# Another order for ScalarE's silu, gelu, sums and evictions in the first feed-forward of a four-stage block

## The reference

```python
def bitlinear158(x, w, b):
    xq = act_quant(rms_norm(x))          # 8-bit integers per row
    wq = weight_quant(w)                 # -1, 0, 1 times a scale
    return einsum('bsd,od->bso', xq, wq) + b
h = silu(bitlinear158(x, w1, b1))        # 512 -> 2048
h = gelu(h, approximate=False)
h = layer_norm(h, ln_g, ln_b)
return bitlinear158(h, w2, b2)           # 2048 -> 512
```

## Time and profile before

| | us |
|---|---|
| median of 3 runs | 903.49 (903.21 to 906.27) |
| the profiled execution | 903.19 |
| its span in the trace | 901.4 |
| busy: PE / DVE / ACT / POOL | 673.6 / 678.6 / 610.7 / 325.6 |

### The profile page before, as it was taken

How to read it: one execution, slowest core, us unless ns; L and a number is a source line. 1 busy time by engine, 2 the same in 40 slices (tenths; PEclk the granted TensorE clock), 3 DMA queues, 4 the chain that set the end, 5 groups by cost and what they waited for, 6 DMA issues and landing times. The chain is left out here.

```text
span 901.4 us, 14255 instructions
## 1 busy us (share of the span) xinstructions
PE 673.6 (75%) x5262; PEld 371.7 (41%) x5262; DVE 678.6 (75%) x1140; ACT 610.7 (68%) x814; POOL 325.6 (36%) x355
## 2 busy tenths in 40 slices
PE   5853056767857757779989978899998377979785
PEld 2421023333423323446655545556355144545452
DVE  1569879999999997885893797556442488989983
ACT  2788459998977894588982886489362055656574
POOL 0012611446295556371671265113031023323332
PEclk9985578999887898679999998999999798989999
DMA  8800030000000000622320121123000000000001
GB/s 320 329 1 0 17 124 0 1 1 1 0 1 1 0 1 2 209 65 96 95 66 28 34 65 45 33 69 107 0 2 1 33 1 12 25 24 23 24 36 47
DMA packets 21761, 43.70 MB, mean 48 GB/s; under 512 B 3905, under 2 KB 8513, under 8 KB 20801
## 3 DMA queue, kind: packets, MB, share of 16 engines
q1 hardware_dynamic: 21696, 42.85, 13.8%
HBM read 38.61 MB, written 4.19 MB: 47 GB/s over the span
## 5 line engine op out<-in xcount | busy, mean ns | idle before, releaser
L1460 DVE TENSOR_REDUCE c_nmax<-c_s 128x1 f32<-128x384 f32 (+3 forms) x176 | 108.7, 633 | 83.5 <-PE c_s L1670 83.5
L1572 ACT ACTIVATE c_probs<-c_e 128x512 f32<-128x512 f32 (+1 forms) x176 | 94.5, 558 | 57.8 <-PE c_e L1700 56.8
L1395 POOL TENSOR_TENSOR c_psum<-c_probs 128x1536 f32<-128x1536 f32 x16 | 55.9, 3492 | 156.4 <-ACT c_probs L1572 156.4
L1168 PE MATMUL b_y<-w2q,b_q2T 128*128 128x512 bf16 x256 | 72.5, 438 | 51.4 <-ACT b_q2T L1093 25.8
L2098 PE MATMUL d_gu<-gateq,d_xqT 128*128 128x352 bf16 x512 | 93.1, 332 | 13.8 <-DVE d_h L1899 12.7
L1667 PE MATMUL c_s<-c_kT,c_qaT 96*128 96x128 f16 (+3 forms) x256 | 73.4, 320 | 22.5 <-DVE c_nmax L1460 20.2
L1142 PE MATMUL b_up<-shared,b_xqT 128*128 128x512 bf16 x256 | 73.5, 414 | 2.4 <-ACT b_h L1059 2.4
L1698 PE MATMUL c_e<-c_qaT,c_kT 98*128 98x512 f16 (+3 forms) x256 | 69.7, 306 | 3.3 <-ACT c_qaT L1559 2.8
L2027 ACT ACTIVATE d_sg<-d_gu,d_dq 128x352 f32<-128x352 f32 x64 | 35.4, 554 | 52.2 <-PE d_gu L2098 52.2
L2098 PEld LDWEIGHTS d_gu<-gateq,d_xqT 128*128 128x128 bf16 x512 | 49.4, 103 | 50.0 <-DVE d_h L1899 19.0
L1168 PEld LDWEIGHTS b_y<-w2q,b_q2T 128*128 128x128 bf16 x256 | 25.6, 108 | 90.0 <-issue 36.5
(11 more groups left out here) (232 smaller groups left out, 1836.0 us busy)
## 6 DMA issues: line engine op xcount, KB each, us to landing
c_stage<-in_gateT SPq DMA_DIRECT2D x16, 704.0 KB, 4.0
c_stage<-in_downT SPq DMA_DIRECT2D x6, 768.0 KB, 4.7
xs<-in_x SPq DMA_DIRECT2D x4, 1024.0 KB, 17.3
a_wf<-in_w1T SPq DMA_DIRECT2D x2, 2048.0 KB, 16.0
a_wf<-in_w2T SPq DMA_DIRECT2D x2, 2048.0 KB, 20.9
out<-xs SPq DMA_DIRECT2D x16, 256.0 KB, 2.0
a_ctxT<-in_ctxT SPq DMA_DIRECT2D x1, 1024.0 KB, 4.9
b_ln_g<-in_ln_g SPq DMA_DIRECT2D x1, 1024.0 KB, 4.8
```

What stands on the lines that cost most here:

```text
L1168: last = nc.tensor.matmul(y_ps[:], q2T[:, n % 2, c, :], w2q[:, c, :], start=(c == 0), stop=(c == IC - 1))
L1395: nc.gpsimd.tensor_tensor(psum[:], region(slot, 0)[:, :, P:], region(slot, 1), ALU.add).then_inc(psum_ready, 1)
L1460: nc.vector.tensor_reduce(nmax[:, G % 2, i, n:n + heads], s_ps[u % 2][:, 0:heads * (i + 1) * P].rearrange("p (n k) -> p n k", n=heads), ax ...
L1572: nc.scalar.activation(probs[:, G % 2, at:at + width], e_ps[fill % 3][:, 0:width], ACT.Exp).then_inc(e_read, 1)
```

## The change

In ACT's loop over the pairs the same steps are called in another order. Before gelu(n) stand now both halves of silu(n) and both of silu(n+1), with squares(n-2) and first_half(n-2) between the latter. gelu(n+1) follows spread(n) directly, and squares(n-1) and gather(n+2) come behind it. No step is added or taken out, and no other stream changes.

```diff
@@ -1099,15 +1099,15 @@
                 n = 2 * p
                 silu(n, 0)
                 silu(n, 1)
+                squares(n - 2)
+                silu(n + 1, 0)
+                first_half(n - 2)
+                silu(n + 1, 1)
                 gelu(n)
-                squares(n - 2)
-                first_half(n - 2)
                 spread(n)
-                silu(n + 1, 0)
+                gelu(n + 1)
                 squares(n - 1)
                 gather(n + 2)
-                silu(n + 1, 1)
-                gelu(n + 1)
                 spread(n + 1)
                 first_half(n - 1)
                 if p == 7:
```

## The result

| | before | after |
|---|---|---|
| median of 8 runs of each, us | 904.09 (903.21 to 910.78) | 910.75 (907.56 to 912.47) |
| ratio after to before, 95% interval | | 1.0057 (1.0029 to 1.0084) |
| profiled execution / its span, us | 903.19 / 901.4 | 912.47 / 910.7 |
| stage length, us | 240.02 | 246.11 |
| ahead of the stage / behind it, us | 119.17 / 542.21 | 122.90 / 541.69 |

A forecast was written before the change was run, and what follows sets the result against it. DVE was taken as the bound, with ACT running ahead of it. Start +3.34, middle -0.38 and last tiles +0.98 gave +3.94, so +4.0 on 903.49: 907.5 us, 0.44% slower; 8-in-10 range 903.3 to 910.8.

The forecast's parts named there:

- ACT's relief is worth 0: Pair loop: 16 table loads fewer, 20.5 us off ACT, booked as 0 because DVE is the bound.
- The start: Tile 0: gelu(0) 4.32 us later behind tile 1's silus; DVE enters the full loop 3.34 us late at affine(1).
- The middle: Tiles 2 to 13: new loop DVE to PE to ACT booked 0; two old deviation waits go, -0.4 (-0.38 in the sum).
- slack at slope(12): Tile 12's turn: gelu's mean ready at 300.07, DVE there at 302.09, so 2.0 us of slack.
- slope(14): Tiles 14 and 15: DVE newly waits 1.54 us for the mean; +0.98 us left by affine(15).
- The tail: Chain from spread(15) to the last two projections: shifts by the same 0.98 us as affine(15).
- rival C: Up projections on PE at 1.2 GHz make the new loop bind in more turns: +6 to +10, say 910.5 us; chance 0.22.
- +4.0: Whole kernel: the summed delay, +3.34 - 0.38 + 0.98 = +3.94, rounded, in us.
- 5.9: Upper bound of the delay in us, 4.32 + 1.54, with no old wait recovered; more only by rival C.
- The total: Whole kernel: 903.49 + 4.0 = 907.5 us, 0.44% slower.
- the forecast's own range: Whole kernel: 906.2 to 908.9 us for the main forecast, which had chance 0.60.
- within 0.5%: Whole kernel: change too small to tell, under 4.5 us (line at 908.0); share 0.52, against 0.41 slower and 0.07 faster.

The follow-up runs named there:

- e5: Kernel before, old order, with Silu in place of Gelu, leaving one table load; computes something else. Ratio to before 0.9961, stage 240.32 us.
- e1: Changed kernel with the old order in the first pair only. Ratio to before 1.0063, stage 243.94 us.
- e2: Kernel before with the new order in the first pair only. Ratio to before 1.0031, stage 243.35 us.
- e4: Changed kernel with the old order in the first and last pair, new in the six between. Ratio to before 1.0006, stage 242.51 us.
- e9: As e4, but gather(n+2) ahead of squares(n-1) in the six middle pairs. Ratio to before 1.0001, stage 240.51 us.
- e8: Changed kernel with 22 spare matmuls on PE in its pause before down(14,0). Ratio to before 1.0032, stage 243.94 us.
- e10w: Kernel before, old order, even tiles' second-half evictions moved from DVE to ACT, 22 spare matmuls before down(14,0). Ratio to before 0.9947, stage 236.81 us.
- e14w: Kernel before, old order, all second-half evictions on ACT, turn_hidden(n-1,1) ahead of turn_inputs(n+3) on PE, spare matmuls in the tail. Ratio to before 0.9983, stage 239.59 us.

## Why the prediction was right, point by point

- **DVE bounds, ACT's relief is worth 0.** Right. The turn is 26.99 against 27.00 us with 23 us less work on ACT over the loop, and e5 with 39 us less takes 194.25 us from affine(1) to affine(15) where before takes 193.97.
- **The start.** Mechanism right, +3.34 forecast at affine(1), +2.97 measured. gelu(0) came 3.94 later instead of 4.32, because PE's clock rose 0.8 us sooner after the first gather in that execution and tile 1's last up projection ended 0.4 us sooner. e1 and e2 isolate it: without it affine(1) is where it was, with it alone the kernel is 0.31% slower.
- **The middle.** Booked 0 and -0.38; measured -0.66 from affine(1) to affine(13) in the changed kernel. The slack at slope(12) was 1.74 us where I had 2.0. But the 0 held by luck: the late gather costs up to 1.5 us of waits where the start is not late (e1, e4, e9), which I had not seen, and in the changed kernel the late start covered them.
- **slope(14).** Forecast a new wait of 1.54, measured 1.30; +0.98 by affine(15), measured 3.27 - 2.31 = +0.96.
- **The tail.** This step failed: "so I shift the tail by the same 0.98" took it for rigid. It is rigid up to down(14,0), 8.8 us behind affine(15) in both kernels; from there the last residual came 2.83 us later still, from PE's clock after a longer pause (e8). I had the clock as rival C, in the wrong place: I looked for it at the up projections. The other parts of the sum were 0.67 us too high together, so +4.0 became +6.1 in the stage. That is above the 5.9 that I had given as the bound without rival C.
- **The total.** 0.44% forecast, 0.57% measured, with 0.44 inside the interval. There is luck in this. The median of the changed kernel, 910.75, is 0.05 us under the top of the range (910.8) and above the forecast's own range (906.2 to 908.9); it sits where I had put rival C. The part of it that the tail's clock makes was in no term of the sum, and part of the distance between the medians may be the first stage's late clock, which has nothing to do with the change. The share given to "within 0.5%" was the larger, and the result lies just past that line; a tail that was costed would have put it there.

## What to carry to other kernels

Count what an engine waits for, not what it does: 20 to 39 us of work taken off an engine that runs ahead of the bound moved nothing inside the loop, while of 4 us put in front of the bound's first instruction 3 were left after the first two tiles and stayed to the end (e2). When a reordering groups steps that share a table, look at the first tile, where nothing hides the later result, and keep the old order there. Use freed time by moving work from the bound to the freed engine, in a place where no one waits for it (e10w), and look at the last pauses of TensorE, where a few us of idle time set the clock for the chain that ends the stage. A filler put there must be over when its successor could start: the same 22 matmuls won 2.85 us in e8 and held the tail up by 0.8 us in e10w and 2.8 in e14w.

## What the runs showed of the hardware

- Being finished earlier can make TensorE slower. In the tail the eight matmuls took 1.89 us after pauses of 2.23 and 2.91 us, 3.17 after one of 2.48, and 3.05 to 3.57 after pauses of 3.15 to 5.70 us (granted clock 1.00 after the pauses of 2.23 and 2.91, 0.57 after that of 2.48, 0.50 after those of 3.15, 5.47 and 5.70); 22 spare matmuls in the pause (4.91 us, then 0.61 idle) brought 1.89 back. The length of the pause alone does not decide it: 2.91 us went well and 2.48 did not.
- The first rise of TensorE's clock moves between executions, and the total with it. The first clock record stands at 12.96 to 15.71 us in eleven of the fourteen profiled executions, and eight f32 matmuls of the first stage took 3.67 us there. It stands at 19.35, 22.61 and 22.76 in the other three (e10w, e1, after), and the same eight took 5.24, 6.56 and 6.68. A window ahead of the first record prints 1.00 all the same. The changed kernel's eight runs lie in two groups, 907.6 to 910.0 and 911.5 to 912.5; whether the first rise parts them is not shown, since one of them was profiled.
- A table load can wait itself. In the changed kernel five loads ahead of a silu had 5.5 us of idle time before them, released by PE, where the loads of before had 0.3 us.
